# One decoder layer: thresholds taken for each FFN matrix by itself, the third matrix prepared first, and all five engines' orders written anew

## The chip, the cores and the metric

One core of one Trainium2 chip runs the kernel in one launch. The metric is the device time of that launch in microseconds (us); lower is better.

## The reference, cut to what matters

The input is x, 8 sequences of 256 rows of 256 numbers. Three sublayers follow each other, each with a residual and a LayerNorm: attention over 64 latent keys with the four largest logits of each head, cross attention over a context of 64 rows, and a gated FFN with ternary weights. The change is in the preparation of the FFN's three matrices and in the scale of its inputs:

```python
def _ternary_quant(w):
    s = jnp.mean(jnp.abs(w))
    wq = jnp.round(jnp.tanh(w / (s + EPS))) * jnp.arctanh(s)
    return w + jax.lax.stop_gradient(wq - w)

def _linear_bit(x, w, g):
    xq = _act_quant(_rmsnorm(x, g))       # 8 bits per row
    wq = _ternary_quant(w)
    return jnp.einsum('bsd,od->bso', xq, wq)

swish = jax.nn.silu(_linear_bit(x, w1, g1))
x_v = _linear_bit(x, w2, g2)
return _linear_bit(swish * x_v, w3, g3)
```

So each matrix needs the sum of its absolute values (one number), a comparison with a threshold from above and one from below, and a factor arctanh(s) that is applied to the activations later.

## The kernel before, in words

The 2048 rows are 16 tiles of 128 rows. Every tile n goes through some thirty small steps, each a Python function of n (L1, max_8, top_4, exp_1, PT1 and so on), and each engine has one list of such calls that is written out by hand: PE in lines 660 to 709, ACT (ScalarE) in 975 to 1022, DVE (VectorE) in 1265 to 1307, POOL (GpSimd) in 1483 to 1510, the DMA queue of SP in 308 to 342. An engine takes its list strictly in order; a call waits on counting semaphores (`a_L1, 1` after a call's own arguments on PE is a wait for a PSUM region to be free). The tables HOME_... say which PSUM banks each call writes.

What bears on the change:

- **Front.** SP loads the inputs in a fixed order. PE combines weight matrices (T1_, T2_, T2T, A_, C_, WF, WB, lines 366 to 445). A_ needs wqx, C_ needs woTx. B_ (551) and L2 (567) are the cross attention's logits; L2(0) needs all four copy_B of the first two sequences from ACT (853). In between, the first tiles go through the first attention.
- **FFN matrices.** w1T, w2T and w3T are loaded last but one (324 to 326), since w1T and w2T reuse space of other weights. sum_abs(w) on ACT (785) sums |w| per partition. One matmul S3 (447) with a matrix of ones adds the three sums over the partitions, after all three sum_abs. thresholds (1067) on DVE makes four rows of three numbers each. ternary(w) (1085) on DVE makes the matrix: one comparison, then a second with a subtraction. centre_3 (1095) on DVE sums the third ternary matrix over its columns and subtracts: one reduce and eight tensor_scalar. Z_ (621) is the first FFN product, O3 (646) the second; pack_h and gain_x(1) wait for ternaries because they reuse the raw matrices' space.
- **arctanh.** ratio_of_means, atanh_series and atanh_weights (1321 to 1350) on POOL, with one logarithm on ACT (794).
- **Variance columns.** square_2(n) on ACT (885) sums squares of a row and then, in an instruction of its own that waits for the first, makes three columns parts2 = eps_parts * var1 + var2. roots_2(n) on POOL (1403) raises them to powers, and scale_x on DVE needs those.
- **Fillers.** warm(count, bank) (355) issues matmuls on zeros: 20 in the front, 39 in the tail.

The order of sum_abs in ACT's list is 2, 1, 0, behind copy_L1(5) and exp_1(4); ternary(0), ternary(1) and ternary(2) stand between the steps of tiles 1 to 8 in DVE's list, and centre_3 right ahead of gate_1(1).

Of the kernel before, what the change touches and what calls it, by code (L numbers as in the profile page):

```python
# [66 lines left out]
HOME_Z2 = (1, 0, 0, 3, 3, 0, 3, 0, 2, 1, 3, 2, 0, 0, 3, 0)
HOME_HT = (4, 5, 2, 7)
HOME_O3 = (4, 4, 4, 0, 2, 2, 2, 6, 1, 6, 7, 0, 2, 5, 7, 2)


def decoder_layer(nc, a, out):

    with ExitStack() as ctx:
# [149 lines left out]
        def bank(table, k):  # L224
# [35 lines left out]
        (g_d4, g_d1, g_spr, g_sc2, g_P1, g_rt1, g_sd1, g_rt2, g_P2, g_lo2, g_xg, g_hg, g_rh, g_rt3) = sems(  # L260
            "g_d4 g_d1 g_spr g_sc2 g_P1 g_rt1 g_sd1 g_rt2 g_P2 g_lo2 g_xg g_hg g_rh g_rt3")
# [15 lines left out]
        def _(sp):  # L277
# [69 lines left out]
        def _(pe):  # L347
# [273 lines left out]
            def Z_(w, n, *freed):  # L621

                bank_of(*freed)
                if n == 0:
                    pe.wait_ge(c_tern, w + 1)
# [34 lines left out]
            warm(9, 0); Q(0); L1(0); warm(11, 2); T1_(0, p_warm, 1); T1_(1, a_L1, 1, v_mask, 1)  # L660
# [51 lines left out]
        def _(act):  # L712
# [172 lines left out]
            def square_2(n):  # L885
# [5 lines left out]
                if n == 0:  # L891
                    act.wait_ge(c_const, 10)
# [685 lines left out]
```

## Time and profile before

| what | value |
| --- | --- |
| median of the runs | 341.74 us (341.0 to 341.8, 3 runs) |
| profiled execution, its own time | 338.98 us |
| its span | 337.2 us, mean granted TensorE clock 0.993 |
| busy share of the span | PE 91%, ACT 83%, DVE 82%, POOL 78% |
| instructions | PE 2368 matmuls, DVE 704, ACT 495, POOL 282 |

Busy is the time in which at least one instruction of the engine is running. Matmuls are pipelined, so a busy PE is not PE at its peak. The span is 1.8 us shorter than the execution's own time, and the execution lies 2.8 us below the median of the runs.

### The profile page before, as it was taken

What the parts mean: (1) busy time and instruction counts of PE and PEld (TensorE: products, weight loads), DVE (VectorE), ACT (ScalarE), POOL (GpSimd) and SP (SyncE); (2) the same over time, 40 slices, a digit from 0 to 9 for tenths busy, and PEclk for the clock granted to TensorE, in tenths of its full rate; (3) what the DMA queues carried; (4) which work ended last, traced back from release to release, by engine and by line L of the source; (5) the groups of instructions that cost most, each with busy time, mean ns of one, the idle gap of its engine ahead of it and who ended that gap; (6) DMA issues with size and microseconds to landing.
All of it is one profiled execution on the core that took longest, in us unless ns stands there. A gap on an engine that the chain in (4) does not pass through costs nothing.

```text
span 337.2 us, 7128 instructions
## 1 busy us (share of the span) xinstructions
PE 306.2 (91%) x2368; PEld 196.8 (58%) x2371; DVE 277.7 (82%) x704; ACT 279.7 (83%) x495; POOL 263.0 (78%) x282
## 2 busy tenths in 40 slices
PE   7788999989898979999999999999999999888882
PEld 3587678444576655564755658565757555555441
DVE  1397426999987799999998999998989999998861
ACT  2569889995468667777997979999899989999994
POOL 3265704889899994999996898999878999988641
PEclk9979999999999999999999999999999999999999
DMA  7999930005103120141030343528436235543011
GB/s 229 231 412 404 405 108 2 1 2 96 29 2 64 32 48 17 33 78 32 18 66 16 64 83 44 94 48 143 80 73 77 56 72 118 110 80 77 1 49 47
DMA packets 58292, 30.67 MB, mean 91 GB/s; under 512 B 53584, under 2 KB 56144, under 8 KB 57168
## 3 DMA queue, kind: packets, MB, share of 16 engines
q1 hardware_dynamic: 58256, 30.22, 36.7%
q8 instruction: 19, 0.31, 0.4%
q14 instruction: 17, 0.14, 0.1%
HBM read 15.01 MB, written 2.10 MB: 51 GB/s over the span
## 4 chain that ended last, share of the span: by engine, by line
PE 47%; ACT 16%; POOL 12%; issue 11%; DMA 7%; DVE 5%; SPq 0%; POOLq 0%; ACTq 0%; DVEq 0%
PE wide L575 10%; PE wide L607 6%; DMA region_c<-in_wkcqT 4%; PE wide L563 4%; PE wide L632 3%; POOL P L1419 3%; PE wide L538 3%; PE wide L495 3%; PE wide L531 3%; PE wide L589 2%; DMA w_raw<-w_raw 2%; ACT region_t L940 2%; PE wide L469 2%; ACT region_c L934 2%; PE wide L507 2%
## 5 line engine op out<-in xcount | busy, mean ns | idle before, releaser
L575 PE MATMUL wide<-B_sb,x1T 128*128 128x512 f32 x128 | 57.9, 597 | 0.8 <-DVE region_c L1218 0.8
L1111 DVE MAX8 m<-Ls 128x8 f32<-128x64 f32 x256 | 34.0, 209 | 14.9 <-ACT Ls L812 14.8
L607 PE MATMUL wide<-V,PT 128*128 128x256 f16 x384 | 44.7, 273 | 0.4 <-DVE V L1154 0.2
L607 PEld LDWEIGHTS wide<-V,PT 128*128 128x128 f16 x384 | 36.8, 98 | 8.9 <-issue 2.3
L1384 POOL TENSOR_TENSOR Ls<-Ls,m 128x1024 f32<-128x1024 f32 x16 | 30.9, 1932 | 10.7 <-DVE m L1111 10.7
L575 PEld LDWEIGHTS wide<-B_sb,x1T 128*128 128x128 f32 x128 | 23.6, 190 | 26.5 <-issue 24.1
L632 PE MATMUL wide<-tern,region_k 128*128 128x512 f16 x128 | 32.6, 380 | 4.1 <-ACT region_k L918 1.7
L1427 POOL TENSOR_TENSOR P<-P 128x1024 f16<-128x1024 f32 x16 | 34.2, 2135 | 1.9 <-ACT P L873 1.9
L1391 POOL TENSOR_TENSOR Ls<-Ls,masks 128x1024 f32<-128x1024 f32 x16 | 35.0, 2188 | 0.3
L1419 POOL TENSOR_TENSOR P<-P,r 128x1024 f32<-128x1024 f32 x16 | 33.5, 2095 | 1.3
L866 ACT ACTIVATE P<-P,tiny 128x1024 f32<-128x1024 f32 x16 | 18.3, 1142 | 9.1 <-DVE P L1168 6.0
L829 ACT ACTIVATE PT<-wide 128x1024 f32<-128x1024 f32 x16 | 16.3, 1020 | 6.7 <-PE wide L495 6.7
L632 PEld LDWEIGHTS wide<-tern,region_k 128*128 128x128 f16 x128 | 11.2, 97 | 18.1 <-issue 2.5
L1218 DVE SCALAR_TENSOR_TENSOR region_c<-region_c,wide 128x1024 f32<-128x1024 f32 x16 | 19.4, 1214 | 1.3 <-ACT region_c L928 1.2
L656 PE MATMUL wide<-tern,w_raw 128*128 128x256 f16 x128 | 16.6, 273 | 3.9 <-ACT w_raw L957 2.7
L1235 DVE TENSOR_REDUCE tiny<-region_t 128x1 f32<-128x1024 f32 x16 | 19.4, 1211 | 0.9 <-POOL region_t L1445 0.7
L1154 DVE TENSOR_TENSOR V<-wide,V 128x1024 f16<-128x1024 f32 x16 | 19.3, 1209 | 0.9 <-ACT V L881 0.9
L1161 DVE TENSOR_REDUCE m<-wide 128x16 f32<-128x1024 f32 x16 | 19.3, 1208 | 0.6 <-PE wide L575 0.5
L1127 DVE TENSOR_TENSOR masks<-wide,m 128x1024 bf16<-128x1024 f32 x16 | 19.4, 1213 | 0.3
L1168 DVE TENSOR_TENSOR P<-wide,m 128x1024 f32<-128x1024 f32 x16 | 19.3, 1208 | 0.2
L1176 DVE TENSOR_REDUCE r<-P 128x16 f32<-128x1024 f32 x16 | 19.3, 1209 | 0.1
L928 ACT ACTIVATE region_c<-wide,tiny 128x1024 f32<-128x1024 f32 x16 | 17.7, 1106 | 2.1 <-PE wide L632 2.0
(202 smaller groups left out, 835.8 us busy)
## 6 DMA issues: line engine op xcount, KB each, us to landing
region_q<-in_wqx SPq DMA_DIRECT2D x1, 2048.0 KB, 19.3
region_c<-in_woTx SPq DMA_DIRECT2D x1, 2048.0 KB, 10.1
out_x<-region_q SPq DMA_DIRECT2D x16, 128.0 KB, 1.9
region_c<-in_wkcqT SPq DMA_DIRECT2D x2, 768.0 KB, 13.5
region_r<-in_t1w SPq DMA_DIRECT2D x1, 1024.0 KB, 9.7
region_r<-in_w1T SPq DMA_DIRECT2D x1, 1024.0 KB, 13.0
region_t<-in_w2T SPq DMA_DIRECT2D x1, 1024.0 KB, 15.0
w_raw<-in_w3T SPq DMA_DIRECT2D x1, 1024.0 KB, 17.0
```

The lines of the kernel that those rows point to most:

```text
L575: mm = pe.matmul(pair(HOME_L2, n)[:, r * 512:(r + 1) * 512], x1T[n % 2][:, k, :], B_sb[:, n // 2 % 2, k, r * 512:(r + 1) * 512], start=(k ...
L607: mm = pe.matmul(bank(HOME_O2, n)[:, 0:D], PT16[n % 2][:, u * PAIRS + c, :], V16[:, b % 2, w, c, :], start=(u == w == c == 0), stop=(u == ...
L632: mm = pe.matmul(pair((HOME_Z1, HOME_Z2)[w], n)[:, r * 512:(r + 1) * 512], xqT[n % 2][:, w * KD + k, :], tern12[:, w, k, r * 512:(r + 1) * ...
L1111: ins = dve.max(m8[n % 2][:, h, :], Ls[n % 2][:, h * L:(h + 1) * L])
L1127: dve.tensor_tensor(top[n % 2].rearrange("p (r h l) -> p r h l", r=4, h=4), four(HOME_L1, n).rearrange("p r (h l) -> p r h l", h=4), by_fo ...
L1154: dve.tensor_tensor(low, pair(HOME_V, 2 * b + half).rearrange("p (r c n) -> p r c n", r=2, c=2), high, ALU.subtract).then_inc((v_VL0, v_VL ...
L1218: dve.scalar_tensor_tensor(th[n % 2], th[n % 2], 1.0, pair(HOME_Z1, n), ALU.add, ALU.mult).then_inc(v_g1, 1)
L1235: dve.tensor_reduce(ch[n][:, 0:1], hg[n % 2], AX, ALU.max, apply_absolute_value=True).then_inc(v_amh, 1)
L1384: pool.tensor_tensor(heads(Ls[n % 2][:]), heads(Ls[n % 2][:]), over_heads(m8[n % 2][:, :, 0:1]), ALU.subtract).then_inc(g_d1, 1)
L1391: pool.tensor_tensor(Ls[n % 2][:], Ls[n % 2][:], top[n % 2], ALU.mult).then_inc(g_P1, 1)
L1419: pool.tensor_tensor(heads(P2_sb[n % 2][:]), heads(P2_sb[n % 2][:]), over_heads(r2[n % 2][:, 0, :].rearrange("p (h o) -> p h o", o=1)), AL ...
L1427: pool.tensor_tensor(P16[n % 2][:, WIDE:2 * WIDE], P2_sb[n % 2][:], P16[n % 2][:, 0:WIDE], ALU.subtract).then_inc(g_lo2, 1)
```

## The change: what it does, and the diff

1. Each matrix has its own S3 matmul (in its own PSUM bank), its own thresholds and its own place in the count of c_abs, c_sum, c_thr, c_mean and c_tern. The turn is matrix 2, then 0, then 1 (`TURN_OF`). thresholds now makes one column at a time: twelve instructions of one column instead of four of three.
2. w3T is loaded behind wv1, ahead of context. SP waits for T1_ and issues w1T ahead of woTx; w2T follows woTx.
3. sum_abs(2) stands on ACT ahead of copy_Q(1), sum_abs(0) between copy_A(0) and copy_A(1), sum_abs(1) ahead of square_1(1). On DVE ternary(2) stands ahead of keep_bias and ternary(0) ahead of residual_1(1), both ahead of max_8(4); ternary(1) stands ahead of largest_x(0).
4. centre_3 is split: the reduce stays on DVE (sum_3, ahead of gate_1(0)); the eight subtractions go to ACT (behind square_1(6)).
5. The variance columns are made by POOL in roots_2, with a wait of POOL for itself in between.
6. All five lists and the bank tables are new. Fillers: 19 in the front, 28 in the tail.

```diff
+TURN_OF = (1, 2, 0)
...
+            sp.dma_start(w3_raw[:], a["w3T"]).then_inc(ld_raw3, 16)
             sp.dma_start(context[:], a["context"]).then_inc(ld_ctx, 16)
             sp.dma_start(xT[:, 1], a["xT"][:, 1]).then_inc(ld_x1, 16)
             sp.dma_start(wqx, a["wqx"]).then_inc(ld_wqx, 16)
             sp.dma_start(wkckv, a["wkckv"]).then_inc(ld_C, 16)
+            sp.wait_ge(p_T1, 2)
+            sp.dma_start(w_raw[0], a["w1T"]).then_inc(ld_raw1, 16)
             sp.wait_ge(p_T2, 1)
             sp.dma_start(woTx, a["woTx"]).then_inc(ld_C, 16)
+            sp.dma_start(w_raw[1], a["w2T"]).then_inc(ld_raw2, 16)
             sp.dma_start(xT[:, 2:4], a["xT"][:, 2:4]).then_inc(ld_x23, 16)
-            sp.wait_ge(p_T1, 2)
-            sp.dma_start(w_raw[0], a["w1T"]).then_inc(ld_raw1, 16)
-            sp.dma_start(w_raw[1], a["w2T"]).then_inc(ld_raw2, 16)
-            sp.dma_start(w3_raw[:], a["w3T"]).then_inc(ld_raw3, 16)
...
-            def S3(*freed):
+            def S3(w, *freed):
...
-                pe.wait_ge(c_abs, 3)
-                pe.matmul(bank(HOME_S3, 0)[:, 0:3], ones[:], prep[:, 0, :], start=True, stop=True
+                pe.wait_ge(c_abs, TURN_OF[w] + 1)
+                pe.matmul(bank(HOME_S3, TURN_OF[w])[:, 0:1], ones[:], prep[:, 0, w:w + 1], start=True, stop=True
...
+            T2T(a_Q, 2); L1(2, v_WF, 1); PT1(1, a_PT1, 1); A_(0, a_T2, 1)
+            A_(1, a_PT1, 2); WT(0, a_A, 1); S3(2); L1(3, a_L1, 3, v_mask, 3)
+            B_(0, 0, v_AT, 1, c_mean, 2); RT(1, a_A, 2); XW(0); C_(0, a_B, 1); S3(0, a_R, 2); O1(0)
...
+            def centre_3():
+
+                act.wait_ge(c_sum3, 1)
+                for c in range(FC):
+                    ins = act.activation(tern3[:, c, :], tern3[:, c, :], ACT.Identity, scale=-float(D),
+                                         bias=tern3_sum[:, c:c + 1])
+                ins.then_inc(c_cent, 1)
...
-                if n == 0:
-                    act.wait_ge(c_const, 10)
-                act.wait_ge(a_sq2, n + 1)
-                act.activation(parts2[n], eps_parts[:], ACT.Identity, bias=var2[n], scale=var1[n]).then_inc(a_mom2, 1)
...
-            def thresholds():
+            def thresholds(w):
...
+                dve.wait_ge(c_sum, TURN_OF[w] + 1)
...
-                dve.wait_ge(c_thr, 2)
-                link(dve.tensor_scalar(dst, w_raw[w], prep[:, 9, w:w + 1], None, ALU.is_lt))
-                dve.scalar_tensor_tensor(dst, w_raw[w], prep[:, 8, w:w + 1], dst, ALU.is_gt,
-                                         ALU.subtract).then_inc(c_tern, 1)
-
-            def centre_3():
-
-                dve.wait_ge(c_tern, 3)
-                link(dve.tensor_reduce(tern3_sum[:], tern3[:], AX, ALU.add))
-                for c in range(FC):
-                    ins = dve.tensor_scalar(tern3[:, c, :], tern3[:, c, :], float(D), tern3_sum[:, c:c + 1],
-                                            ALU.mult, ALU.subtract)
-                ins.then_inc(c_cent, 1)
+                dve.wait_ge(c_thr, 2 * TURN_OF[w] + 2)
+                upper, lower = (prep[:, 8, w:w + 1], ALU.is_gt), (prep[:, 9, w:w + 1], ALU.is_lt)
+                first, second = (upper, lower) if w == 2 else (lower, upper)
+                link(dve.tensor_scalar(dst, w_raw[w], first[0], None, first[1]))
+                dve.scalar_tensor_tensor(dst, w_raw[w], second[0], dst, second[1], ALU.subtract).then_inc(c_tern, 1)
+
+            def sum_3():
+
+                dve.wait_ge(c_tern, 1)
+                dve.tensor_reduce(tern3_sum[:], tern3[:], AX, ALU.add).then_inc(c_sum3, 1)
...
-                pool.wait_ge(c_mean, 2)
+                pool.wait_ge(c_mean, 6)
...
-                pool.wait_ge(a_mom2, n + 1)
+                pool.wait_ge(a_sq2, n + 1)
+                pool.tensor_scalar(parts2[n], eps_parts[:], var1[n], var2[n], ALU.mult, ALU.add).then_inc(g_mom2, 1)
+                pool.wait_ge(g_mom2, n + 1)
                 pool.tensor_tensor(roots2[n], parts2[n], three_roots[:], ALU.pow).then_inc(g_rt2, 1)
```

## Rows read from the trace of the kernel before

**Rows 1.** Busy time by stretch: PE, weight load, DVE, ACT, POOL; clock; DMA.

```profile
0.00:20.00 20.00, 14.93 (x152) 10.09 (x154) 7.38 (x41) 8.81 (x17) 5.86 (x26) 0.97 0.91 256
20.00:60.00 40.00, 39.15 (x386) 30.14 (x384) 22.66 (x77) 33.97 (x69) 21.78 (x21) 0.97 0.62 249
60.00:160.00 100.00, 91.03 (x642) 55.65 (x642) 91.99 (x215) 72.54 (x120) 89.32 (x100) 1.00 0.19 37
160.00:300.00 140.00, 135.85 (x1022) 86.20 (x1020) 131.35 (x322) 131.75 (x231) 125.77 (x119) 1.00 0.40 72
300.00:337.20 37.20, 25.25 (x178) 14.69 (x177) 24.27 (x54) 32.67 (x61) 20.31 (x20) 0.99 0.21 50
```

**Rows 2.** Instructions that write the ternary matrices: ns min/median/max, first and last start us.

```profile
L1100 DVE TENSOR_SCALAR tern<-tern,tern_sum x8: 279/281/288, 129.4 to 130.8; 128x256 f16<-128x256 f16 x8
L791 ACT ACTIVATE tern<-w_raw x1: 1912/1912/1912, 60.1 to 60.1; 128x2048 f16<-128x2048 f32 x1
...
L1091 DVE TENSOR_SCALAR tern<-region_r,prep x1: 3050/3050/3050, 75.4 to 75.4; 128x2048 f16<-128x2048 f32 x1
L1092 DVE SCALAR_TENSOR_TENSOR tern<-region_r,prep,tern x1: 2350/2350/2350, 78.5 to 78.5; 128x2048 f16<-128x2048 f32 x1
L1091 DVE TENSOR_SCALAR tern<-region_t,prep x1: 1309/1309/1309, 92.6 to 92.6; 128x2048 f16<-128x2048 f32 x1
...
L1091 DVE TENSOR_SCALAR tern<-w_raw,prep x1: 1278/1278/1278, 107.5 to 107.5; 128x2048 f16<-128x2048 f32 x1
L1092 DVE SCALAR_TENSOR_TENSOR tern<-w_raw,prep,tern x1: 3871/3871/3871, 108.8 to 108.8; 128x2048 f16<-128x2048 f32 x1
```

**Rows 3.** One POOL instruction beside ternary(0) (timeline), and its group's mean.

```profile
77.34 1.71 POOL L1396 TENSOR_TENSOR tiny<-tiny,two_roots 128x2 f32<-128x2 f32 x1
...
L1396 POOL TENSOR_TENSOR tiny<-tiny,two_roots 128x2 f32<-128x2 f32 x16 | 12.3, 769 | 0.4 <-ACT junk L843 0.4
```

**Rows 4.** PE's timeline ahead of L2(0): start us, us, line, names, count.

```profile
54.99 1.09 PE L495 MATMUL wide<-ident,Ls 128*128 128x128 f32 x8
...
56.06 0.42 PE L547 MATMUL wide<-ident,y_rows 128*128 128x128 f32 x2
...
57.28 0.73 PE L483 MATMUL wide<-lat_k,QT 32*128 32x128 f32 x16
57.94 1.13 PE L538 MATMUL wide<-woT,AT 128*128 128x256 f32 x4
58.90 7.03 PE L575 MATMUL wide<-B_sb,x1T 128*128 128x512 f32 x16
```

**Rows 5.** ACT's timeline: copy_B(3, 0), the last operand of L2(0).

```profile
55.10 1.02 ACT L858 ACTIVATE B_sb<-wide 128x1024 f32<-128x1024 f32 x1 [0.32 <-PE wide L563]
```

**Rows 6.** ACT's timeline in the tail, around one variance column instruction.

```profile
281.89 0.19 ACT L889 ACTIVATION_READ_ACCUMULATOR junk<-region_q 128x1 f32 x1
282.11 0.39 ACT L894 ACTIVATE tiny<-eps_parts,tiny 128x3 f32<-128x3 f32 x1
282.41 1.09 ACT L928 ACTIVATE region_c<-wide,tiny 128x1024 f32<-128x1024 f32 x1
```

**Rows 7.** Instruction groups nearest to the new forms: busy, mean ns | idle before.

```profile
L767 ACT ACTIVATE C_sb<-wide,row_mean 128x256 f32<-128x256 f32 x8 | 3.1, 474 | 0.1
...
L1334 POOL TENSOR_SCALAR prep<-prep 128x3 f32<-128x3 f32 x7 | 1.6, 227 | 0.6
```

**Rows 8.** DMA: SP's issue of w1T (start us); sizes and us to landing.

```profile
24.11 0.43 SPq L324 DMA_DIRECT2D region_r<-in_w1T  x1
...
region_c<-in_woTx SPq DMA_DIRECT2D x1, 2048.0 KB, 10.1
...
region_r<-in_w1T SPq DMA_DIRECT2D x1, 1024.0 KB, 13.0
```

**Rows 9.** A stretch of 2 us at the lower clock, and T2_'s matmuls around it.

```profile
20.00:22.00 2.00, 2.00 (x22) 2.00 (x21) 1.56 (x2) 1.11 (x3) 2.00 (x2) 0.50 1.02 424
...
L387 PE MATMUL wide<-region_c,region_t x64: 272/348/422, 17.8 to 23.0; 96*64 96x128 f32 x64
```

More of the change, by code:

```diff
@@ L624, in Z_ @@
                 if n == 0:
-                    pe.wait_ge(c_tern, w + 1)
+                    pe.wait_ge(c_tern, TURN_OF[w] + 1)
                 if n < TURNED:
@@ new lines, in _ @@
+            L1(1, a_L1, 1, v_mask, 1); T2_(a_T1, 2); RT(0, a_T1, 1); WF(v_mask, 2); Q(1, a_T2k, 1)
+            PT1(0, a_R, 1); T2T(a_Q, 2); L1(2, v_WF, 1); PT1(1, a_PT1, 1); A_(0, a_T2, 1)
+            A_(1, a_PT1, 2); WT(0, a_A, 1); S3(2); L1(3, a_L1, 3, v_mask, 3)
+            B_(0, 0, v_AT, 1, c_mean, 2); RT(1, a_A, 2); XW(0); C_(0, a_B, 1); S3(0, a_R, 2); O1(0)
+            C_(1, a_L1, 4, v_mask, 4); B_(1, 0); WB(a_C, 1); WT(1, c_mean, 4); Q(2); XW(1, a_C, 2); S4()
+            PT1(2, v_AT, 2, v_y1, 1); RT(2, c_sqk, 1); B_(2, 0, a_B, 2); X1T(0, a_Q, 3); O1(1)
@@ L1018, in _ @@
[L1018 to L1021 removed]
+            copy_Q(0); copy_L1(0); copy_T1(0); spread_lat_v(); copy_T1(1); copy_L1(1); exp_4(0); exp_1(0)
@@ new lines, in _ @@
+            centre_wo(); exp_1(1); keep_T2(); copy_R(0); sum_abs(2); copy_Q(1); copy_PT1(0); exp_4(1)
+            copy_T2(); copy_L1(2); copy_PT1(1); copy_A(0); sum_abs(0); copy_A(1); copy_L1(3)
+            copy_B(0, 0); copy_R(1); exp_4(2); exp_1(2); square_kv(); copy_C(0); copy_C(1); square_C()
+            copy_B(1, 0); copy_Q(2); copy_PT1(2); copy_R(2); copy_X1(0); exp_4(3); copy_B(2, 0)
+            copy_L1(4); copy_B(3, 0); square_1(0); sum_abs(1); square_1(1); exp_1(3); exp_1(4)
+            high_V(0, 0); exp_4(4); copy_X1(1); exp_2(0); copy_Q(3); copy_PT1(3); copy_L1(5); copy_PT1(4)
@@ new lines, in _ @@
+            square_1(2); high_P(0); copy_X1(2); copy_L1(6); copy_Q(4); copy_R(3); exp_2(1); high_V(1, 0)
+            exp_1(5); exp_4(5); high_V(0, 1); exp_4(6); high_P(1); copy_R(4); exp_1(6); high_V(1, 1)
+            exp_2(2); copy_PT1(5); copy_R(5); copy_X1(3); copy_L1(7); square_2(0); log_ratio()
+            square_2(1); copy_PT1(6); copy_B(0, 1); copy_B(1, 1); copy_B(2, 1); square_1(3); high_P(2)
+            copy_L1(8); exp_2(3); whole_x(0); pack_x(0); copy_R(6); exp_1(7); copy_Q(5); copy_B(3, 1)
@@ new lines, in _ @@
+            whole_h(0); exp_1(10); square_1(7); copy_X1(7); copy_L1(11); whole_x(3); square_2(4)
+            pack_h(0); exp_2(6); exp_4(10); copy_B(0, 2); copy_B(1, 2); copy_B(2, 2); tanh(2); exp_4(11)
+            exp_2(7); copy_B(3, 2); pack_x(3); copy_R(9); copy_PT1(10); exp_1(11); high_P(6); copy_L1(12)
+            copy_X1(8); whole_x(4); high_P(7); pack_x(4); whole_h(1); square_3(0); tanh(3); square_2(5)
+            high_V(1, 3); square_h(2); square_1(8); copy_R(10); pack_h(1); tanh(4); square_h(3)
@@ L1264, in _ @@
             link(dve.memset(y1_rows[:, :, D:D + 1], (D * LN_EPS) ** 0.5))
-            spread_lat_k(); max_8(0); top_4(0); max_8(1); sum_4(0); top_4(1); rope(); max_8(2); top_4(2)
-            sum_4(1); max_8(3); top_4(3); sum_4(2); keep_W1(); scale_AT(0); keep_bias(); residual_1(0)
-            scale_AT(1); max_8(4); residual_1(1); scale_AT(2); top_4(4); keep_squares(); sum_4(3)
-            sum_4(4); residual_1(2); max_8(5); top_4(5); max_2(0); sum_4(5); shift_2(0); max_2(1)
-            shift_2(1); thresholds(); sum_2(0); scale_AT(3); low_V(0, 0); sum_2(1); residual_1(3)
@@ L1307, in _ @@
-            moments_3(14); residual_3(15); moments_3(15)
+            spread_lat_k(); max_8(0); top_4(0); max_8(1); sum_4(0); top_4(1); keep_W1(); rope(); max_8(2)
+            top_4(2); sum_4(1); scale_AT(0); thresholds(2); max_8(3); top_4(3); sum_4(2); thresholds(0)
+            ternary(2); keep_bias(); scale_AT(1); residual_1(0); keep_squares(); ternary(0)
+            residual_1(1); max_8(4); scale_AT(2); top_4(4); max_2(0); shift_2(0); thresholds(1)
+            low_V(0, 0); residual_1(2); sum_4(3); sum_4(4); sum_2(0); max_8(5); top_4(5); max_2(1)
@@ new lines, in _ @@
+            shift_2(1); max_8(6); top_4(6); sum_2(1); low_V(1, 0); low_V(0, 1); scale_AT(3); max_2(2)
+            residual_1(3); sum_4(5); shift_2(2); low_V(1, 1); residual_2(0); sum_2(2); scale_AT(4)
+            sum_4(6); max_8(7); top_4(7); max_2(3); shift_2(3); residual_2(1); scale_AT(5); ternary(1)
+            largest_x(0); scale_x(0); residual_1(4); max_8(8); top_4(8); residual_1(5); sum_2(3)
+            scale_AT(6); sum_3(); gate_1(0); gate_2(0); residual_1(6); residual_2(2); largest_x(1)
```

396 lines of the change are left out of this document (185 added, 211 removed).

## The prediction, made before the changed kernel was run

> **What bounds the kernel now.** I read the table of busy time by stretch first [rows 1]. No engine bounds all of it. In the first 20 us PE is busy 14.93: it waits for loads. From 20 to 60 PE is busy 39.15 of 40, while DVE is busy only 22.66 and POOL 21.78. From 60 to 160 the picture turns: DVE is busy 91.99 of 100 and POOL 89.32, and PE, which had been full, loses 8.97. From 160 to 300 PE is at 135.85 of 140, so it loses 4.15 in 140, a third of the earlier rate. In the last 37.2 us PE is busy 25.25 (fillers included) and ACT 32.67; ACT's idle time lies nearly all behind the last tiles. So: PE bounds 20 to 60 and 160 to 300, ACT the end, and from 60 to 160 the work is held up by DVE and POOL together.
>
> The second view is that of the ternary matrices [rows 2]. All of their DVE work lies inside 60 to 160: ternary(0) at 75.4 takes 3.05 + 2.35 = 5.40, ternary(1) at 92.6 takes 1.31 + 2.35 = 3.66 (its second pass is of the same shape as that of ternary(0)), ternary(2) at 107.5 takes 1.28 + 3.87 = 5.15, and the eight subtractions at 129.4 take 1.66 from first start to last end (129.4, to 130.8 plus 0.28). So some 14.2 us of DVE work without the reduce stand where DVE is short, and none where DVE is idle (17.3 us of idle time between 20 and 60).
>
> **Ternaries 2 and 0 move ahead of max_8(4).** They leave the stretch behind 60 and enter the one before it: 5.40 + 5.15 = 10.55. With the subtractions, which go to ACT, DVE sheds 12.2 us behind 60. What that is worth is bounded above by PE's idle time in the stretch, 8.97, since PE has no less work there, and below by 0: if the idle time comes from the order of the steps, a freer DVE only waits more. Between the ends I take the rate of the nearest stretch that has the same pipeline without any ternary, 160 to 300: 4.15 / 140 = 3.0% idle, so 3.0 of 100 us instead of 8.97, a gain of **6.0**. The twelve one-column thresholds instead of four cost DVE 8 more tiny instructions; I cost them at nothing, as two sets of them lie in the idle 20 to 60.
>
> Of the six passes, two took far longer than their like: 3.05 against 1.31 and 3.87 against 2.35, and a POOL instruction at 77.34, beside ternary(0), took 1.71 where its group has a mean of 0.77 [rows 2, 3]. So the two engines block each other there, and early ternaries, with POOL half idle, would take nearer 3.65 each. I credit this only inside the 6.0. The Trainium skill's page "SBUF — State Buffer", section "Who interferes with whom", says that the port pair shared by VectorE and GpSimd is an exclusive lock, so whichever comes second waits for the whole instruction. This rule also speaks against the change: it puts sixteen more POOL instructions where each can be caught behind a DVE pass. By the rule, with 0.94 us lost each time as in [rows 3], that would be 16 x 0.94 = 15 us of POOL time, against 3.6 by the row of small POOL instructions below.
>
> **The front.** Ahead of L2(0) in PE's list the new order drops PT1(3), X1T(1), L1(5), O1(2) and one filler, and adds two S3. From starts to following starts these are about 1.0, 0.3, 0.7 and 1.0 [rows 4]; with the filler and the S3 about offsetting, PE has 3.0 less to do, and L2(0), which starts at 58.90, could start at 55.9. But L2(0) needs copy_B(3, 0), which ends at 56.1 now [rows 5], and ACT now gets two sum_abs of 1.91 ahead of it [rows 2] and sheds one exp pass of about the length of the copy in [rows 5], 1.0: 2.8 later, 58.9, unless ACT's idle time (6.03 between 20 and 60) swallows it. So L2(0) starts between 55.9 and 58.9, while the steps that were moved behind it (3.0) are still owed. The loss is between 0 and 3.0. I take **2.0**, near the upper end, since sum_abs(0) stands between the two copy_A and so in the line that leads to B_ and L2. If DVE too is behind (ternary(2) is ahead of residual_1(0)), the wait is X1T's and part of the same 3.0.
>
> **Loads.** w3T is 1024 KB, ahead of context, wqx and wkckv; w1T goes ahead of woTx. Before, w1T was issued at 24.11 and landed 13.0 later, at 37.1, behind woTx [rows 8]. That is the row with which to price 1 MB: woTx of 2 MB and x of 0.5 MB stood ahead of it, so 3.5 MB in 13 us or less, at most 3.7 us for each MB. Context, wqx and wkckv then come at most 3.7 us later, woTx at most 7.4. What hides this: rope's DVE work is put behind keep_W1; A_(0) follows T2T, Q(1) and WF; and C_(0) has A_(1), WT(0), B_(0, 0), two RT and XW(0) put ahead of it. I take 0, and keep up to 4 us of loss for the range.
>
> **Variance columns and subtractions.** The instruction on ACT takes from about 281.99, where the reading of the accumulator lets the next one start, to 282.41: 0.42 [rows 6]. Sixteen are 6.7 us of ACT. Eleven or so lie ahead of 280, where PE is the limit; I cost them at nothing. The four of tiles 12 to 15 lie where ACT never pauses: 4 x 0.42 = **1.7** gained. On POOL 16 x 0.227 = 3.6 us are added [rows 7], four of them in the tail, where POOL is busy 20.31 of 37.2, and the hop from ACT to POOL is gone; cost 0, bounds -2 and +2. Eight subtractions on ACT are 8 x 0.47 = 3.8 [rows 7], while ACT is busy 72.54 of 100 in that stretch [rows 1]. They stand ahead of high_V(0, 2) and wait for DVE's sum_3. Covered by ACT's 27 us of idle time; without cover 3.8.
>
> **Sum.** 6.0 - 2.0 + 1.7 = 5.7 us. The profiled execution took 338.98, its span 337.2; the new one would take 333.3. The median lies 2.76 above the profiled execution, so 341.74 - 5.7 = **336.0**.
>
> **Rivals.**
> (A) *DVE was the whole cause.* PE's idle time behind 60 goes nearly all, 8 of 8.97, the front costs nothing, the tail gives 1.7: 341.7 - 9.7 = 332.0. For it: 12.2 us shed against 8.97 lost. Against it: POOL, busy 89.32, gets work rather than loses it. Chance 0.20, for times below 333.
> (B) *The order is the cause.* Only 2.0 of the 6.0 comes, the front costs 2.0, the tail gives 1.7: 340.0; with nothing from the tail 341.7. POOL's 89% and the hand-written order on five engines speak for it: relief on one passes the wait to the next. Chance 0.15.
> (C) *Slower: w1T comes late.* sum_abs(0) stands in ACT's list ahead of copy_A(1), copy_L1(3) and copy_B(0, 0), and S3(0) in PE's ahead of O1(0) and C_(1). The forecast has it land earlier than now: w3T is ahead of it, woTx and x are not, 1.5 MB less or some 5 us. If it lands no earlier than now, at 37.1, ACT and PE stand still together for up to 4 us, woTx, which lands 10.1 after its issue now, is up to 7.4 late [rows 8], and PE, full from 20 to 60, cannot make it good. With 3.0 in the front, 4 by the loads, and the 6.0 not earned because tiles 4 and 5 start late: 341.7 + 3.0 + 4 - 1.7 = 347; with a third of the 6.0 earned 345. It decides from a landing of w1T at about 36 on. Chance 0.15.
> (D) *The lower clock in the tail.* Fillers in the tail go from 39 to 28. The granted clock is 0.50 (the 1.2 GHz level) at 20 to 22 us, after PE had waited for T2_'s weights, and T2_'s matmuls there range from 272 to 422 ns [rows 9], a factor of 1.55. PE is busy 25.25 of the last 37.2; for the last 10 us that is 6.8, which would take 3.7 longer: 336.0 + 3.7 = 339.7. Chance 0.08. The Trainium skill's page "TensorE: Matmul & The Clock Gate", section "What's actually happening", says that the throttled state is the default and that activity releases it; by it fewer fillers are a risk, unless the new order leaves fewer gaps, and the sum would be 339.7 rather than 336.0.
> That the parts do not do what they say is not a rival: they are plain.
>
> **How the numbers follow.** Forecast (333 to 339) 0.42; A 0.20; B 0.15; C 0.15; D 0.08. A measurement of this kernel tells about 0.3% (1.0 us) from no change. Faster (under 340.7): 0.42 + 0.20 + 0.08 and a third of B, 0.75. Same: 0.10 (the rest of B). Slower: 0.15. The range is 331.0 to 343.0: it takes in most of A, all of B and D, and ends between B and C, so that C (0.15) and the lower end of A (0.05) are left out.
>
> **What would show it.** Right: L2(0) starts within 2 us of 58.9; PE's idle time from 60 to 160 falls to about 3 us; three ternaries of 3.7 to 4 us, two before 56; no POOL power takes 1.7; ACT has no gap around the tail's square_2. Wrong: a wait of PE for sum_abs's S3 or for woTx of over 1 us (C); PE's idle time behind 60 as before with waits on POOL (B); a clock below 1.00 behind 300 (D).

## The result: 328.2 us, faster than the range, and the profile after

| what | before | changed |
| --- | --- | --- |
| median of the runs | 341.74 us | 328.17 us (3 runs) |
| profiled execution, its own time | 338.98 us | 328.17 us |
| its span | 337.2 us | 326.4 us |

The ratio is 0.9593 [0.9543, 0.9642], 4.1% faster. The forecast was 336.0, the range 331 to 343. Ratios here compare fast runs alone: of the three runs of the changed kernel, 333.08 was a slow one and is not in the ratio. From one profiled execution to the other the change gained 10.8 us, where the sum said 5.7. Measured twice more, the changed kernel had 329.34 and 327.25 us beside 339.51 and 339.03 us of the kernel before on the same chip (ratios 0.9717 [0.9665, 0.977] and 0.9614 [0.9573, 0.9656]). So the gain is 10 to 12 us, and the 341.74 was a little high.

Busy time by stretch of the changed kernel, with the columns of [rows 1]:

```profile
0.00:20.00 20.00, 15.28 (x178) 10.74 (x180) 7.86 (x41) 10.17 (x20) 7.04 (x25) 1.00 0.91 267
20.00:60.00 40.00, 37.70 (x348) 26.83 (x344) 26.75 (x79) 35.87 (x68) 24.20 (x23) 1.00 0.60 244
60.00:160.00 100.00, 97.12 (x772) 64.14 (x765) 89.71 (x238) 81.05 (x135) 94.48 (x112) 1.00 0.23 39
160.00:300.00 140.00, 135.23 (x974) 85.06 (x973) 132.85 (x317) 129.36 (x231) 130.39 (x129) 1.00 0.41 77
300.00:326.40 26.40, 15.05 (x108) 8.35 (x107) 14.75 (x31) 22.06 (x37) 11.56 (x13) 0.93 0.09 31
```

PE's idle time from 60 to 160 fell from 8.97 to 2.88, by 6.1, as forecast. Yet the whole gained more. Over the span PE is idle 26.0 us (326.4 less the sum of its busy times, 300.4) instead of 31.0, and busy 300.4 instead of 306.2. So 5.0 us of the 10.8 are idle time and 5.8 are busy time, which the forecast had held constant. T2_ took 3.74 us instead of 5.43, because its clock did not fall this time (rows below): that 1.7 is luck and not the change. The fillers, 47 instead of 59, were busy 13.4 us instead of 15.3. The rest, some 2.2, is not traced to single steps.

The new places of the steps on DVE and ACT (timelines; start us, duration us), for [rows 2]:

```profile
41.01 1.69 DVE L1101 TENSOR_SCALAR tern<-w_raw,prep 128x2048 f16<-128x2048 f32 x1
42.73 3.90 DVE L1102 SCALAR_TENSOR_TENSOR tern<-w_raw,prep,tern 128x2048 f16<-128x2048 f32 x1
49.23 1.28 DVE L1101 TENSOR_SCALAR tern<-region_r,prep 128x2048 f16<-128x2048 f32 x1
50.54 2.35 DVE L1102 SCALAR_TENSOR_TENSOR tern<-region_r,prep,tern 128x2048 f16<-128x2048 f32 x1
95.48 1.28 DVE L1101 TENSOR_SCALAR tern<-region_t,prep 128x2048 f16<-128x2048 f32 x1
...
109.12 2.27 DVE L1107 TENSOR_REDUCE tern_sum<-tern 128x8 f32<-128x2048 f16 x1
122.06 3.29 ACT L807 ACTIVATE tern<-tern,tern_sum 128x256 f16<-128x256 f16 x8
```

Ternary(2) and ternary(0) lie before 56. The former takes 5.59, where it had 5.15 in its old place; ternary(0) takes 3.63 instead of 5.40. What POOL ran beside them (its timeline), for [rows 3]:

```profile
41.56 2.92 POOL L1389 TENSOR_TENSOR Ls<-Ls,m 128x1024 f32<-128x1024 f32 x1
44.45 2.34 POOL L1374 TENSOR_TENSOR d<-m 128x64 f32<-128x64 f32 x1
...
49.39 4.06 POOL L1361 TENSOR_TENSOR v_scale<-v_scale,two_roots 128x2 f32<-128x2 f32 x2 [2.27 <-DVE v_scale L1091]
...
96.90 2.99 POOL L1413 TENSOR_TENSOR tiny<-tiny,three_roots 128x3 f32<-128x3 f32 x1
99.86 0.29 POOL L1374 TENSOR_TENSOR d<-m 128x64 f32<-128x64 f32 x1
```

The blocking did not end with the move. A small instruction of L1374 took 2.34 us at 44.45, and 0.29 at 99.86 with no ternary beside it; two powers took 4.06, and one beside ternary(1) 2.99. In a later run without ternaries beside them (tern_late, below) the same two powers took 0.70 and 0.72. But between 20 and 60 us POOL has idle time to pay it with, 15.8 of 40.

PE's timeline ahead of L2(0), for [rows 4, 9], and what it waited for (in brackets: idle us before, and what ended it). The first line is T2_ in the kernel before, the others are of the changed kernel:

```profile
17.80 5.43 PE L387 MATMUL wide<-region_c,region_t 96*64 96x128 f32 x64 [2.27 <-DMA region_c<-in_wkcqT]
...
17.00 3.74 PE L389 MATMUL wide<-region_c,region_t 96*64 96x128 f32 x64 [2.46 <-DMA region_c<-in_wkcqT]
24.68 1.97 PE L471 MATMUL wide<-front 128*128 128x256 f32 x8 [1.80 <-DMA front<-in_xT]
38.25 1.95 PE L424 MATMUL wide<-region_c,region_k 128*64 128x256 f32 x16 [0.43 <-DMA region_c<-in_woTx]
55.89 3.60 PE L577 MATMUL wide<-B_sb,x1T 128*128 128x512 f32 x8
```

L2(0) starts at 55.89, the lower bound of 55.9 to 58.9. S3 has no wait over 1 us. The wait of 1.80 us for x's second block is new: the kernel before has none there. The DMA view, for [rows 8] (KB, median us from issue to landing):

```profile
region_c<-in_woTx SPq DMA_DIRECT2D x1, 2048.0 KB, 17.4
w_raw<-in_w3T SPq DMA_DIRECT2D x1, 1024.0 KB, 16.8
region_r<-in_w1T SPq DMA_DIRECT2D x1, 1024.0 KB, 19.3
```

w1T was issued at 13.93 and landed at 33.2, 3.9 earlier than before; woTx was issued at 20.77 and landed at 38.2, 4.8 later, which cost PE the 0.43 above.

**A ruler that leaves the front out.** Some executions have a stretch of 3.4 to 10.2 us at the granted clock of 0.50 near 14 to 25 us and some have none; the three profiles of the changed kernel start L2(0) at 55.89, 57.04 and 58.88. From L2(0) to the end they take 270.5, 270.7 and 270.1. So below I give, beside the ratio, the span behind L2(0), against a mean of 270.4. Of the kernel before it is 278.3 (337.2 - 58.90), but there the 3.0 us of steps that the change moved behind L2(0) are done ahead of it. With them it would be up to 281.3. Two limits of this ruler: it stands on one profiled execution of each kernel, and the clock in the middle and in the tail is still inside it. The same stretch in three parts, cut at the starts of L2(0), L2(7) and L2(15) (busy time as above), first before and then changed:

```profile
58.90:155.30 96.40, 87.43 (x617) 53.74 (x616) 88.26 (x215) 69.56 (x113) 85.71 (x96) 1.00 0.20 38
155.30:284.80 129.50, 126.80 (x961) 80.52 (x959) 121.09 (x294) 120.72 (x215) 117.04 (x113) 1.00 0.38 68
284.80:337.20 52.40, 39.00 (x261) 22.85 (x263) 39.16 (x86) 47.77 (x86) 33.58 (x33) 0.99 0.26 58
```

```profile
55.90:148.30 92.40, 89.75 (x681) 58.01 (x679) 81.18 (x217) 74.10 (x124) 86.46 (x104) 1.00 0.20 37
148.30:271.20 122.90, 121.80 (x913) 77.92 (x911) 117.80 (x287) 112.83 (x197) 116.50 (x116) 1.00 0.39 71
271.20:326.40 55.20, 39.95 (x272) 23.14 (x268) 40.86 (x90) 49.64 (x88) 36.81 (x38) 0.97 0.28 62
```

The first part has more matmuls (681 against 617) in 4.0 us less; the second fewer (913 against 961), and PE's idle time in it fell too, from 2.70 to 1.10. The orders differ, so only kernels of one order can be compared part by part.

### The profile page after: what moved, and what is told of

It reads as the page before. It is cut to its first block, busy times and chain, and to the rows that moved or that the text cites. A ratio compares the mean times of both kernels' runs of the same rounds, so it can differ in the third digit from the quotient of the medians.

```text
span 326.4 us, 7130 instructions
## 1 busy us (share of the span) xinstructions
PE 300.4 (92%) x2363; PEld 195.1 (60%) x2363; DVE 271.9 (83%) x704; ACT 278.5 (85%) x487; POOL 267.7 (82%) x298
## 4 chain that ended last, share of the span: by engine, by line
PE 34%; POOL 30%; issue 12%; DMA 10%; ACT 9%; DVE 4%; SPq 1%; POOLq 0%; ACTq 0%; DVEq 0%
PE wide L577 8%; DMA region_c<-in_woTx 5%; PE wide L609 5%; DMA region_c<-in_wkcqT 4%; POOL Ls L1389 4%; POOL Ls L1396 4%; POOL P L1426 4%; PE wide L634 3%; POOL P L1434 3%; PE wide L591 2%; ACT region_t L948 2%; POOL tiny L1413 2%; PE wide L540 2%; PE wide L533 2%; POOL region_t L1452 2%
## 5 line engine op out<-in xcount | busy, mean ns | idle before, releaser
L1396 POOL TENSOR_TENSOR Ls<-Ls,masks 128x1024 f32<-128x1024 f32 x16 | 34.1, 2137 | 3.4 <-ACT Ls L834 3.1
L1389 POOL TENSOR_TENSOR Ls<-Ls,m 128x1024 f32<-128x1024 f32 x16 | 31.9, 1997 | 4.0 <-DVE m L1116 4.0
L1426 POOL TENSOR_TENSOR P<-P,r 128x1024 f32<-128x1024 f32 x16 | 30.5, 1904 | 1.3
L885 ACT ACTIVATE P<-P 128x1024 f16<-128x1024 f32 x16 | 16.8, 1053 | 6.2 <-POOL P L1426 6.2
L1452 POOL TENSOR_TENSOR region_t<-region_c,region_q 128x1024 f32<-128x1024 f32 x8 | 16.0, 2000 | 5.4 <-DVE region_c L1234 5.3
L824 ACT ACTIVATE Ls<-wide 128x1024 f32<-128x1024 f32 x16 | 16.3, 1021 | 4.3 <-PE wide L485 4.2
```

What stands on the lines that cost most here:

```text
L1389: pool.tensor_tensor(heads(Ls[n % 2][:]), heads(Ls[n % 2][:]), over_heads(m8[n % 2][:, :, 0:1]), ALU.subtract).then_inc(g_d1, 1)
L1396: pool.tensor_tensor(Ls[n % 2][:], Ls[n % 2][:], top[n % 2], ALU.mult).then_inc(g_P1, 1)
L1426: pool.tensor_tensor(heads(P2_sb[n % 2][:]), heads(P2_sb[n % 2][:]), over_heads(r2[n % 2][:, 0, :].rearrange("p (h o) -> p h o", o=1)), AL ...
L1452: pool.tensor_tensor(hg[n % 2], hh[n % 2], g3, ALU.mult).then_inc(g_hg, 1)
```

## The experiments

Nearly all of them are the changed kernel with one part undone, so that the new order stays. First its repeat, unedited.

> The changed kernel once more, beside the kernel before. Theory T (the ternary work left the stretch in which VectorE is short) and theory O (the new order, not the parts, made the time) both expect a ratio of 0.955 to 0.965. Theory F (the profiled execution of before had a poor front: its clock stood at 0.50 around 20 us, and that of the changed kernel did not) expects a ratio nearer 0.97 to 0.975 here, and T2_'s 64 matmuls to take either about 3.7 us or about 5.4 us from one profile to the next.

Measured: 329.34 us, ratio 0.9717, where theory F had put it; the third measurement had 0.9614, where T and O had. No stretch at 0.50 in the front, 270.7 behind L2(0). T2_ took 3.73 us here and 5.90 in the third measurement's profile.

**Variance columns back to ScalarE.** In square_2:

```diff
+                act.wait_ge(a_sq2, n + 1)
+                act.activation(parts2[n], eps_parts[:], ACT.Identity, bias=var2[n], scale=var1[n]).then_inc(g_mom2, 1)
```
and the TENSOR_SCALAR is taken out of POOL's roots_2.

> The changed kernel with the variance columns made by ScalarE again, in square_2, all orders as changed. By the prediction's term (4 x 0.42 us in the tail) 1.7 us slower than the changed kernel, between 1 and 3. If ScalarE is a limit over the whole second half, up to 16 x 0.42 = 6.7 us slower. If GpSimd is now the limit, as its 94% from 60 to 160 us suggests, no slower or 1 to 3 us faster.

Measured: 329.61 us, ratio 0.9674 [0.9608, 0.974], beside 329.34 of the repeat; 270.1 behind L2(0). The move is worth nothing that can be seen. The medians alone, with runs from 326.0 to 332.15, could not tell 1.7 us from 0. The stretch behind L2(0) can, if its 0.6 us of spread holds here too, and it speaks against the step's gain of 1.7.

**Subtractions back to VectorE, behind the reduce.**

```diff
-                dve.tensor_reduce(tern3_sum[:], tern3[:], AX, ALU.add).then_inc(c_sum3, 1)
+                link(dve.tensor_reduce(tern3_sum[:], tern3[:], AX, ALU.add))
+                for c in range(FC):
+                    ins = dve.tensor_scalar(tern3[:, c, :], tern3[:, c, :], -float(D), tern3_sum[:, c:c + 1],
+                                            ALU.mult, ALU.add)
+                ins.then_inc(c_cent, 1)
```
and centre_3() is taken out of ScalarE's list.

> The changed kernel with the eight subtractions of the third matrix on VectorE again, right behind the reduce. They take 1.66 us there; ScalarE gets 3.2 us (the span of its eight) back. Theory T: 0 to 1.7 us slower. Theory O: within 1 us of the changed kernel.

Measured: 336.43 us, ratio 0.9825 [0.978, 0.987]; the profiled execution, 336.43 too, has 277.4 behind L2(0), 7.0 lost. That is more than any theory gave, but it is not the same in every execution: the nine runs go from 331.73 to 338.33, and by the ratios (0.9825 against the repeat's 0.9717) the loss is 3.7 us. The two shortest, 331.73 and 331.92, had a mean clock of 0.984, the profiled one 0.969. The eight themselves (ns min/median/max, first and last start) and, from the timelines, what ran on POOL meanwhile and what PE then waited for; the last three lines are busy time by stretch:

```profile
L1109 DVE TENSOR_SCALAR tern<-tern,tern_sum x8: 274/281/1957, 112.9 to 115.9; 128x256 f16<-128x256 f16 x8
...
113.36 1.98 POOL L1393 TENSOR_TENSOR Ls<-Ls,m 128x1024 f32<-128x1024 f32 x1
...
115.82 1.94 POOL L1430 TENSOR_TENSOR P<-P,r 128x1024 f32<-128x1024 f32 x1
...
120.41 1.97 PE L497 MATMUL wide<-ident,Ls 128*128 128x128 f32 x8 [3.49 <-DVE region_c L1238]
...
119.00:126.00 7.00, 5.59 (x27) 3.68 (x28) 5.51 (x26) 3.41 (x6) 4.24 (x4) 0.51 0.21 41
57.33:155.87 98.54, 92.52 (x681) 59.60 (x680) 86.15 (x225) 71.11 (x116) 87.16 (x105) 0.97 0.20 35
324.00:326.00 2.00, 2.00 (x10) 1.29 (x9) 0.53 (x2) 2.00 (x4) 0.54 (x1) 0.50 0.06 16
```

They took 4.98 us and not 1.66: one had 1957 ns, and the last, which started at 115.9, ended at 117.85 with the POOL instruction of 1.94 us that ran beside it. gate_2(0) (L1238) started at 119.09 instead of 113.70, 4.0 late when measured from L2(0). PE stood 3.49 us, and its clock was then 0.50 for 6.8 us (the window from 119 to 126). From L2(0) to L2(7) the 681 matmuls take 98.5 instead of 92.4, so 6.1 of the 7.0 are lost here: 3.4 as idle time, 2.8 as busy time at the lower clock. The tail (from L2(15)) is 1.1 longer, with 3.4 us at 0.50 from 324 on while PE still worked, which the changed kernel's profile did not have. The Trainium skill's page "SBUF — State Buffer", section "Who interferes with whom", says that a tensor_scalar in a two-port mode and a GpSimd instruction exclude each other for a whole instruction. The two durations, 1957 ns and 1.98 us, agree with it.

**Ternaries back to their late places.** ternary(2) stands ahead of low_V(1, 1) and ternary(0) ahead of sum_4(6) in VectorE's list:

```diff
-            ternary(2); keep_bias(); scale_AT(1); residual_1(0); keep_squares(); ternary(0)
+            keep_bias(); scale_AT(1); residual_1(0); keep_squares()
...
-            residual_1(3); sum_4(5); shift_2(2); low_V(1, 1); residual_2(0); sum_2(2); scale_AT(4)
-            sum_4(6); max_8(7); top_4(7); max_2(3); shift_2(3); residual_2(1); scale_AT(5); ternary(1)
+            residual_1(3); sum_4(5); shift_2(2); ternary(2); low_V(1, 1); residual_2(0); sum_2(2); scale_AT(4)
+            ternary(0); sum_4(6); max_8(7); top_4(7); max_2(3); shift_2(3); residual_2(1); scale_AT(5); ternary(1)
```

> The changed kernel with ternary(2) moved to just ahead of low_V(1, 1) and ternary(0) to just ahead of sum_4(6), so that 9.2 us of VectorE work (5.59 + 3.63 by the trace of the changed kernel) are again behind 60 us. Theory T: 5 to 9 us slower than the changed kernel, and TensorE's idle time from 60 to 160 us back at 8 us or more. Theory O: 0 to 3 us slower.

Measured: 336.14 us, ratio 0.9897 [0.9863, 0.9932]; 277.7 behind L2(0), so 7.2 lost. The table by stretch:

```profile
58.30:156.50 98.20, 90.09 (x682) 58.19 (x681) 88.56 (x222) 73.97 (x125) 92.21 (x104) 1.00 0.18 35
325.00:327.00 2.00, 1.76 (x9) 1.26 (x10) 0.21 (x1) 2.00 (x5) 0.14 (x1) 0.50 0.19 66
```

PE's idle time between L2(0) and L2(7) is 8.1 instead of 2.7, and the same 682 matmuls take 98.2 instead of 92.4, so 5.8 are lost here. Another 1.4 stand in the tail, where the clock was again 0.50 for 3.4 us, from 325 on. The two ternaries had short durations there (1.28 + 2.37 and 1.29 + 2.35, 7.3 in all). So they cost PE 5.8 of their 7.3 us: in the new order VectorE has little slack in this stretch. Theory T holds. Whether the early places would pay in the old order too was not run.

**The order alone**: the three edits above together.

> The new order alone: thresholds, loads, banks and all lists of the changed kernel, but with the variance columns on ScalarE, the eight subtractions on VectorE behind the reduce, and both early ternaries back at their late places. Theory P (the parts make the gain, and add up): tern_late lost about 6.8 us against the changed kernel, cent_back about 7.0 (some of it by the clock), mom_back nothing; together 12 to 14 us above the changed kernel's 329.3, so 341 to 343, a ratio of 1.005 to 1.012 to the kernel before, and PE's idle time from 60 to 160 is 12 us or more. Theory L (the two losses overlap, since both are paid out of the same short stretch of VectorE): ratio 0.985 to 1.000, idle 8 to 11. Theory O (the order itself is the gain): ratio under 0.98, as the changed kernel.

Measured: 338.49 us, ratio 0.9956 [0.9916, 0.9997], and 281.0 behind L2(0). Its stretch and its longest wait:

```profile
54.50:157.00 102.50, 92.00 (x681) 59.05 (x680) 93.61 (x230) 72.22 (x121) 91.43 (x101) 0.98 0.19 33
...
122.60 1.41 PE L497 MATMUL wide<-ident,Ls 128*128 128x128 f32 x8 [3.62 <-DVE region_c L1242]
```

So the parts together are worth 10.5 (281.0 - 270.4) in the new order, and the order by itself next to nothing: 281.0 lies within the 278.3 to 281.3 of the kernel before, and the whole run is 0.4% shorter. Theory O has fallen, and rival B, by which only 2.0 of the idle time would come, with it. Of the 10.5, 10.1 are lost between L2(0) and L2(7) (102.5 against 92.4): 7.9 as PE's idle time (10.5 against 2.65) and 2.3 as busy time (92.00 against 89.75, of which a stretch of 3.4 us at 0.50 behind the wait of 3.62 explains at most 1.7).

The ratio and the idle time lie in theory L's ranges. But the overlap is small. Between L2(0) and L2(7) the single losses are 5.8 and 6.1, together 11.9, and both edits at once lose 10.1: they overlap by 1.8, and cent_back had 6.8 us at the lower clock where order_only had 3.4. In PE's idle time it is 5.5 and 3.4 against 7.9, an overlap of 1.0.

**The subtractions alone, in the old order.** The kernel before, with the eight on ScalarE behind square_1(5):

```diff
-            copy_L1(9); square_h(0); copy_Q(5); square_1(5); high_P(4); copy_Q(6); exp_4(8); square_2(3)
+            copy_L1(9); square_h(0); copy_Q(5); square_1(5); centre_3(); high_P(4); copy_Q(6); exp_4(8); square_2(3)
```

> The kernel before, with only the eight subtractions moved to ScalarE (the third ternary matrix negated, as in the changed kernel), behind square_1(5) in its list; nothing else is changed. The eight took 1.66 us on VectorE there. Theory U (their price depends on what stands beside them; here GpSimd did not block them): a gain of 0 to 1.7 us, ratio 0.995 to 1.000. Theory W (eight subtractions on VectorE are worth 4 us or more wherever they stand, as cent_back suggested): ratio 0.988 or less. Slower (over 1.003) if ScalarE's 3.8 us are not covered there.

Measured: 341.3 us, ratio 1.0013 [0.9978, 1.0047]. The move by itself gains nothing in the old order. Theory W is refuted; U had said 0.995 to 1.000 and is met within the interval. Whether VectorE gained something that ScalarE's eight then took back, the run does not show.

**The subtractions on VectorE at another place.** The first of two runs puts them behind scale_AT(8) in VectorE's list:

> The changed kernel with the eight subtractions on VectorE again, but not behind the reduce at 112 us ahead of gate_1(0): they stand some 25 us later, behind scale_AT(8), where O3(0), their only reader, is still over 10 us away. Theory G (cent_back lost its time because gate_2(0) came directly behind the eight, PE waited 3.5 us for it and the clock then fell): now within 2 us of the changed kernel, ratio 0.970 to 0.978, no lower clock between 100 and 160 us. Theory K (GpSimd is busy over 90 of 100 in this stretch, so that the eight are blocked wherever they stand, and each us of VectorE counts here): the eight take 4 us or more again, and the ratio is 0.980 to 0.987.

Measured: 339.41 us, ratio 0.9964 [0.9927, 1.0001]. I had read the list wrongly: that place comes at 161 us, and their reader O3(0) stands at 158 in PE's list. PE stood still for them:

```profile
167.79 1.87 PE L658 MATMUL wide<-tern,w_raw 128*128 128x256 f16 x8 [8.08 <-issue]
```

The run decides nothing between G and K; it shows only that a stall of PE is not made good behind it (280.8 behind L2(0), 10.4 lost). The second run has the right place:

```diff
-            scale_x(2); max_8(10); top_4(10); low_V(0, 3); max_2(6); shift_2(6); residual_2(4)
+            scale_x(2); centre_3(); max_8(10); top_4(10); low_V(0, 3); max_2(6); shift_2(6); residual_2(4)
```

> The eight subtractions on VectorE once more, now between scale_x(2) and max_8(10), at about 139 us. O3(0), their only reader, starts at 157.95 in the changed kernel, so there are 18 us to spare (sub_late had them behind scale_AT(8), which ends after that: PE stood still for O3(0), and that run says nothing of GpSimd). Theory G (cent_back lost its time because gate_2(0) came directly behind the eight, PE waited 3.5 us for it and the clock fell): within 2 us of the changed kernel, ratio 0.965 to 0.975, and no clock of 0.50 between 100 and 180 us. Theory K (GpSimd is busy over 90 of 100 here, so the eight are blocked wherever they stand, and VectorE has no slack): they take 4 us or more, and the ratio is 0.980 or more.

Measured: 329.6 us, ratio 0.97 [0.9657, 0.9743]; the repeat beside it had 327.25 and 0.9614, so the whole times leave up to 2.9 us open, and the repeats of the changed kernel themselves go from 327.25 to 329.34. In its profile it takes 270.5 behind L2(0), the changed kernel 270.4: nothing lost. The eight, and POOL meanwhile:

```profile
L1113 DVE TENSOR_SCALAR tern<-tern,tern_sum x8: 278/279/307, 140.0 to 141.4; 128x256 f16<-128x256 f16 x8
...
139.90 0.34 POOL L1419 TENSOR_SCALAR tiny<-eps_parts,tiny 128x3 f32<-128x3 f32 x1
140.32 1.01 POOL L1421 TENSOR_TENSOR tiny<-tiny,three_roots 128x3 f32<-128x3 f32 x1
```

Theory G: by the profiles the same work on the same engine costs 7.0 at 113 us and nothing at 140. At 140 only small POOL instructions stood beside it, and no step for which PE waits stood behind it. The run changes both at once, so it does not tell which of them counts more. K's first half (blocked wherever they stand) is refuted.

**The fillers of the tail**: one in each of the six groups instead of 3, 5, 6, 4, 6 and 4.

```diff
-            warm(6, 0); HT(12, v_g1, 15); Z_(1, 15, v_g2, 15); O3(12, v_g1, 16); HT(13)
+            warm(1, 0); HT(12, v_g1, 15); Z_(1, 15, v_g2, 15); O3(12, v_g1, 16); HT(13)
```

> The changed kernel with one filler matmul in each of its six tail groups instead of 28 in all. The fillers compute nothing, so the output is whole. Rival D (the tail lives on its fillers): the granted clock falls to 0.50 in the tail ahead of PE's last work, and the whole is 2 to 4 us slower than the changed kernel, ratio 0.973 to 0.985. Rival E (in the last 20 us PE waits for ScalarE and VectorE after every step and at the lower clock would still wait): the clock falls, but the time stays within 1 us, ratio 0.963 to 0.972.

Measured: 328.8 us, ratio 0.9698 [0.9653, 0.9742], 1.5 over the median of the repeat beside it (2.8 by the ratios). The clock did fall, to 0.50 from 296.7 to 300.1 and from 306.9 to 317.1 us, and the profiled execution takes 272.7 behind L2(0), 2.3 more:

```profile
306.90:317.10 10.20, 7.99 (x37) 4.39 (x38) 6.64 (x13) 9.44 (x15) 6.92 (x7) 0.50 0.04 14
```

Between D and E: 1.5 to 2.8, less than the 3.7 that rival D charged; PE still waits in between (it is busy 7.99 of 10.20 at the low clock). With its 28 fillers the changed kernel held 1.00 until PE's last work. But cent_back and tern_late have the same 28 and had 3.4 us at 0.50 there, so they do not make it certain.

**The load of x's second block first** (it is 256 KB in the DMA view, not the 0.125 MB that my expectation said):

```diff
+            sp.dma_start(xT[:, 1], a["xT"][:, 1]).then_inc(ld_x1, 16)
             sp.dma_start(w3_raw[:], a["w3T"]).then_inc(ld_raw3, 16)
             sp.dma_start(context[:], a["context"]).then_inc(ld_ctx, 16)
-            sp.dma_start(xT[:, 1], a["xT"][:, 1]).then_inc(ld_x1, 16)
```

> The changed kernel with the load of x's second block (0.125 MB of the queue) ahead of w3T and the context instead of behind them. In the changed kernel PE waits 1.8 us for it at Q(1). Theory Q (that wait is a real loss of the front): the wait goes, L2(0) starts about 1.5 us earlier, at 54.4, and the whole is 1 to 1.8 us shorter, ratio 0.966 to 0.969 where the changed kernel had 0.9717 by its repeat. Theory N (another load is late next: the context of L1, or woTx at C_(0), or the work behind is limited by GpSimd and ScalarE anyway): the wait goes or moves, and the ratio stays 0.970 to 0.974.

Measured: 327.62 us, ratio 0.9628 [0.956, 0.9697]. It is 1.7 us shorter than the repeat of another set; so it was run again beside a repeat.

> x1_first once more, with more rounds and beside a repeat of the changed kernel. Theory Q (the 1.8 us wait for the load was a loss of the front that lasts to the end): 1.2 us or more shorter than the repeat of the changed kernel beside it, L2(0) earlier by about as much when no lower clock stands in the front of either. Theory N (another wait takes its place): within 0.7 us of it.

> The changed kernel, unchanged, as the other side of x1_again and as a third measurement of the change. Going by the first two, 328.2 and 329.3: 327.5 to 329.5, ratio to the kernel before 0.962 to 0.971; slower by 1.2 us than x1_again by theory Q, within 0.7 by theory N.

Measured: 329.11 us (0.9696 [0.9652, 0.9741]) and 327.25 us (0.9614). It is 1.9 longer than the repeat beside it, so the 1.7 of the first time lay within the spread between sets. The wait of 1.8 us at Q(1) is gone from its profile, and T2_ ahead of it waits 4.01 us instead of 1.66 in the repeat's:

```profile
20.05 5.40 PE L389 MATMUL wide<-region_c,region_t 96*64 96x128 f32 x64 [4.01 <-DMA region_c<-in_wkcqT]
```

L2(0) starts at 58.3 against 58.9. Theory Q is refuted. It is N's mechanism, another wait in its place, though its 0.7 us was missed. No version of these beats the changed kernel.

## Why the prediction was right in direction and wrong in size

**The ternaries and the 12.2 us that DVE sheds: undersized.** This term, +6.0, is the step that failed. Where it was read it came true: PE's idle time from 60 to 160 fell from 8.97 to 2.88, and what stayed is the 3% that I had taken. But I had called that idle time the upper bound of what the edits are worth, and it is not. order_only, the new order with them undone, is 10.5 longer behind L2(0) in the profiles. The stretch left out idle time behind it: between L2(7) and L2(15) PE lost 2.70 in the kernel before and 1.10 in the changed one, and I had held that part constant. And 2.3 of the 10.5 is busy time of PE, in part the lower clock behind a long wait. The kernel before was never below 1.00 from 60 to 160 [rows 1], so that part of the 10.5 belongs to the new order with its parts undone. How much the two ternaries would gain in the old order stays open.

The working has a slip besides: the "some 14.2 us of DVE work" from 60 to 160 is the three ternaries alone (5.40 + 3.66 + 5.15). With the eight subtractions it is 15.9. No term was worked out from it.

**The front, -2.0: about the right size, by another cause, and hidden by luck.** From the end of T2_ to the start of L2(0) the kernel before takes 35.7 us (23.23 to 58.90). The three profiles of the changed kernel take 35.2, 34.6 and 32.8. So the moved steps' 3.0 came nearly in full only in the last one. In the first, PE waits 2.2 us for loads there; in the last its only wait is one of 0.15. In the profile of the result this cost 2.5 of the 3.0, and that L2(0) stands at 55.89 even so is the earlier and faster T2_ (0.8 and 1.7 us). I had charged the 2.0 to the two sum_abs ahead of copy_B on ACT, but the 32.8 has both of them too and loses next to nothing.

**Loads at 0: wrong in the profile of the result.** w1T landed 3.9 earlier (the forecast said some 5) and S3 waited for nothing, so rival C fell. But PE waits 0.43 for woTx and 1.80 for x's second block, which the change put behind w3T in the queue. x1_again, which takes the 1.80 away, is no faster.

**The variance columns, +1.7: wrong.** mom_back has them on ACT again and loses nothing behind L2(0). That ACT never pauses in a stretch did not mean that each of its instructions sets the end.

**The subtractions at cost 0 on ACT: right, and the reason incomplete.** ACT covered them (8 in 3.29 us). What they were worth on DVE I had put at their duration of 1.66, inside the 6.0. The move is worth nothing in the old order (b_cent_act), nothing against a place at 140 us (sub_mid), and 3.7 (ratios) to 7.0 (profile) against one behind the reduce in the new order (cent_back). I had named the blocking of [rows 3] and charged it to no step that stays on DVE.

**The rivals.** A (332.0, below 333) came nearest by its time. It charged 8 of the 8.97 of idle time, which was 6.1, and 1.7 for the tail, which was 0, so its sum is no better founded than mine. It is right that DVE's work made nearly all of the gain, and its doubt, that POOL at 89% gets more work, was not borne out: POOL rose to 94.5 of 100 and PE lost less. B fell by order_only, C by the landings, D by the clock of 1.00 up to PE's last work, and few_warm shows that its mechanism is real at 1.5 to 2.8 us instead of 3.7.

**What was to be seen.** L2(0) within 2 us of 58.9: missed by 1 (57.04 and 58.88 in the other two profiles are within it). Idle of about 3: 2.88. No POOL power of 1.7: wrong, the new order has longer ones (4.06 for two, and 2.99), beside the ternaries still. Three ternaries of 3.7 to 4: 5.59, 3.63 and 3.63. No gap of ACT around the tail's square_2: it came so. By the median of the kernel before (341.74, where three later sets of runs have 339.5, 339.8 and 339.0) the forecast was 2 us too high before any step.

## What to carry to other kernels

Price a step by what stands behind it and beside it, and not by its duration: the same eight instructions cost up to 7 us at one place, with a step for which the busiest engine waits behind them and long GpSimd instructions beside them, and nothing at a place with neither. Idle time of a window bounds a gain only if busy time, order and the idle time outside it stay as they are. Where two parts relieve the same engine, undo them one by one and together (5.8 and 6.1 made 10.1 here). And measure from a landmark behind the noisy front: there single profiles of one kernel agreed within 0.6 us, while medians differed by 2. But look at the clock behind the landmark too: a stretch at 0.50 in the tail made 1.1 to 1.4 us in two of the runs.

## What the runs showed of the hardware

The granted clock in the front differs between executions of one and the same kernel: none of it, 3.4, 6.8 or 10.2 us at 0.50 between 14 and 25 us. In the tail, with the same fillers, it was 1.00 up to PE's last work in one profile (changed) and 0.50 for 3.4 us before it in others (cent_back, tern_late). Where PE had waited 3.5 to 8.1 us for one step in the middle (cent_back, order_only, sub_late), 3.4 to 6.8 us at 0.50 followed in the profiles, each time. The Trainium skill's page "TensorE: Matmul & The Clock Gate", section "What's actually happening", says that activity releases a throttle that is the default; that it falls behind a long wait agrees with it.

Short fp16 tensor_scalar instructions on VectorE of some 280 ns were stretched to at most 1957, 2035 and 2167 ns in the three kernels that had them beside GpSimd tensor_tensor instructions (the last while one of 2.12 us ran at 165.29), and stayed at 307 at most where only small ones were near:

```profile
L1113 DVE TENSOR_SCALAR tern<-tern,tern_sum x8: 270/274/2035, 114.9 to 119.8; 128x256 f16<-128x256 f16 x8
...
L1113 DVE TENSOR_SCALAR tern<-tern,tern_sum x8: 274/346/2167, 161.0 to 167.4; 128x256 f16<-128x256 f16 x8
...
165.29 2.12 POOL L1442 TENSOR_TENSOR P<-P 128x1024 f16<-128x1024 f32 x1
```

(The first is of order_only, the others are of sub_late.) Each of these longest durations is within 0.05 us of the GpSimd instruction beside it, and the whole eight took 4.98, 5.11 and 6.67 us instead of 1.66 to 1.68.
